# Two attention layers on one core: turned blocks loaded by whole sequences in rows of 2 KB

## The reference, cut to what matters

```python
x = x + L0_xattn(layernorm(x), ctx, ctx, ...)   # 16 heads of 8
x = x + L0_ffn(layernorm(x), ...)               # 8 experts, top 2
x = x + L1_xattn(layernorm(x), ctx, ...)        # 16 heads of 64
x = x + L1_ffn(layernorm(x), ...)
```

## Time and profile before

| | |
|---|---|
| median of three runs | 915.78 us (908.65 to 916.7) |
| profiled execution | 913.91 us, span 912.3 us |
| TensorE matmul busy | 828.5 us, 91% |
| ScalarE / VectorE busy | 74% / 70% |
| mean granted TensorE clock | 0.974 of full |
| bytes moved by DMA | 171.93 MB, 60.0% of the engines' time on SP's queue |

### The profile page before, as it was taken

The page is one execution under the profiler, slowest core; times in us unless marked ns, Lnnn a source line. Parts: engine busy times, 40 slices in busy tenths (PEclk is TensorE's granted clock), DMA queues, the critical chain, the costliest instruction groups (busy, mean ns, idle before and its releaser), DMA issues.

```text
span 912.3 us, 28139 instructions
## 1 busy us (share of the span) xinstructions
PE 828.5 (91%) x7885; PEld 734.4 (80%) x7885; DVE 638.7 (70%) x2052; ACT 673.3 (74%) x2662; POOL 453.2 (50%) x765
## 2 busy tenths in 40 slices
PE   5899999999998877999999678999999999999985
PEld 3677777777776766999999577889999999999974
DVE  5888887887887743222222578788898888888872
ACT  2999899899898852333334798899888888888860
POOL 3135445444454362111113777788777777776540
PEclk9999999999999997999999899999999999999987
DMA  5897667667767702222222198889899999999871
GB/s 169 247 244 217 204 208 227 201 211 228 219 208 240 196 30 78 70 71 70 70 70 64 64 253 253 253 240 269 246 241 232 238 238 237 240 239 240 240 233 41
DMA packets 160451, 171.93 MB, mean 188 GB/s; under 512 B 16052, under 2 KB 139318, under 8 KB 160374
## 3 DMA queue, kind: packets, MB, share of 16 engines
q1 hardware_dynamic: 153474, 156.77, 60.0%
q0 software_dynamic: 6112, 13.90, 5.7%
q10 hardware_dynamic: 788, 0.39, 0.2%
HBM read 90.87 MB, written 80.13 MB: 187 GB/s over the span
## 4 chain that ended last, share of the span: by engine, by line
PE 67%; DMA 9%; issue 8%; DVE 6%; SPq 4%; POOL 3%; ACT 3%; another core or an unknown queue 0%; POOLq 0%; DVEq 0%; ACTq 0%
PE bank L1233 8%; PE bank L1420 8%; PE bank L1392 7%; PE bank L1399 7%; PE bank L1442 5%; PE bank L1516 4%; PE bank L1432 4%; PE bank L1225 4%; DMA PTC<-turned_blocks 3%; PE bank L1506 3%; PE bank L1187 3%; PE bank L1344 3%; PE bank L1304 2%; PE bank L1521 2%; ACT PR L699 2%
## 5 line engine op out<-in xcount | busy, mean ns | idle before, releaser
L699 ACT ACTIVATE PR<-PR,nmx 128x128 f32<-128x128 f32 x512 | 198.4, 393 | 13.7 <-DVE nmx L898 13.6
L699 ACT ACTIVATE PR<-bank,nmx 128x128 f32<-128x128 f32 x512 | 188.0, 432 | 0.4 <-DVE nmx L898 0.4
L347 POOL TENSOR_TENSOR PR<-PR,rden 128x512 f32<-128x512 f32 x128 | 133.1, 1052 | 50.4 <-DVE rden L903 49.8
L699 ACT ACTIVATION_READ_ACCUMULATOR PR<-bank,nmx 128x1 f32 x512 | 139.6, 273 | 0.0
L1420 PE MATMUL bank<-XCT,wqk 128*128 128x128 f32 x832 | 104.6, 280 | 10.0 <-ACT XCT L687 9.7
L793 ACT ACTIVATE H<-bank 128x512 f32<-128x512 f32 x70 | 41.8, 597 | 92.3 <-PE bank L1392 92.3
L1420 PEld LDWEIGHTS bank<-XCT,wqk 128*128 128x128 f32 x832 | 98.3, 193 | 13.5 <-ACT XCT L687 10.5
L699 ACT ACTIVATION_READ_ACCUMULATOR PR<-PR,nmx 128x1 f32 x512 | 98.2, 192 | 0.0
L1187 PEld LDWEIGHTS bank<-ident,PR 128*128 128x128 f32 x512 | 60.2, 141 | 39.6 <-issue 38.1
L1065 DVE STREAM_TRANSPOSE BT<-PR 128x512 f32<-128x512 f32 x128 | 89.7, 701 | 2.3 <-POOL PR L347 1.5
L898 DVE TENSOR_REDUCE nmx<-bank 128x4 f32<-128x512 f32 x128 | 86.2, 673 | 4.5 <-PE bank L1225 3.5
(11 more groups left out here) (186 smaller groups left out, 1986.1 us busy)
## 6 DMA issues: line engine op xcount, KB each, us to landing
turned_blocks<-BT SPq DMA_DIRECT2D x64, 512.0 KB
PTC<-turned_blocks SPq DMA_DIRECT2D x256, 128.0 KB, 4.2
second_layer_values<-wide SPq DMA_DIRECT2D x32, 512.0 KB
wide<-second_layer_values SPq DMA_DIRECT2D x32, 512.0 KB
expert_outputs<-HF SPq DMA_DIRECT2D x32, 256.0 KB
expert_outputs<-HF SPq DMA_DIRECT2D x64, 128.0 KB
KBD<-expert_outputs SPq DMA_DIRECT2D x64, 128.0 KB
QS<-expert_outputs SPq DMA_DIRECT2D x32, 256.0 KB
```

Of the source, the lines that this page charges most:

```text
L347: nc.gpsimd.tensor_tensor(unit, unit, rden[:, p, G * g:G * g + G].unsqueeze(2).broadcast_to([P, G, P]), ALU.mult).then_inc(s["nm"], 1)
L699: last = nc.scalar.activation(PR[:, g, j * P:(j + 1) * P], scored, ACT.Exp, bias=nmx[:, p, h:h + 1], accum_out=den[:, p, h:h + 1])
```

## The change

`BT`, `PTC` and the DRAM buffer get one layout for the whole sequence: for each block column j, all 16 heads follow each other (2 KB). A half is then four pieces of 1 KB in a row, so each store has rows of 1 KB (512 in place of 128), strided by 2 KB on both sides. The loads are four in place of eight for a sequence, each of 256 KB with rows of 2 KB (128 rows, as before). They wait for both stores and for all products with v of the sequence that used the buffer before, and count on `pt0` alone. TensorE's `values(p, 0)` thus waits for the whole sequence, and the wait on `pt1` falls. The count of instructions on the compute engines stays the same.

```diff
-        bt_dram = nc.dram_tensor("turned_blocks", (2, 2, P, 2 * G * P), FP32, kind="Internal").ap()
+        bt_dram = nc.dram_tensor("turned_blocks", (2, P, 4 * G * P), FP32, kind="Internal").ap()
-        PTC = sb("PTC", [P, 2, 2, 4, 2 * G, 32])
+        PTC = sb("PTC", [P, 2, 4, NH, 32])
-        BT = sb("BT", [P, 2, 2 * G * P])
+        BT = sb("BT", [P, 4, NH * 32])
             def store_blocks(m, p, half):
-                wait_apart(sp, (c["bt"], NU * m + 2 * half + 2), (c[f"pt{half}"], 64 * (m - 1)))
-                sp.dma_start(bt_dram[p, half], BT[:, half, :]).then_inc(c[f"bw{half}"], 16)
-            def load_turned(m, p, half):
-                wait_apart(sp, (c[f"bw{half}"], 16 * (m + 1)), (c["pv"], NU * (m - 2) + 2 * half + 2))
+                wait_apart(sp, (c["bt"], NU * m + 2 * half + 2), (c["pt0"], 64 * (m - 1)))
+                columns = slice(2 * G * 32 * half, 2 * G * 32 * half + 2 * G * 32)
+                sp.dma_start(bt_dram[p].rearrange("r (j c) -> r j c", j=4)[:, :, columns], BT[:, :, columns]).then_inc(c[f"bw{half}"], 16)
+            def load_turned(m, p):
+                wait_apart(sp, (c["bw0"], 16 * (m + 1)), (c["bw1"], 16 * (m + 1)), (c["pv"], NU * (m - 1)))
                 for j in range(4):
-                    sp.dma_start(PTC[32 * j:32 * j + 32, p, half, :, :, :].rearrange("a i h b -> a i (h b)"),
-                                 bt_dram[p, half].rearrange("(i a) (j c) -> j a i c", a=32, j=4)[j]).then_inc(c[f"pt{half}"], 16)
+                    sp.dma_start(PTC[32 * j:32 * j + 32, p, :, :, :].rearrange("a i h b -> a i (h b)"),
+                                 bt_dram[p].rearrange("(i a) (j c) -> j a i c", a=32, j=4)[j]).then_inc(c["pt0"], 16)
 # SP, step1
-                    load_turned(n - 1, q, 0)
-                    load_turned(n - 1, q, 1)
+                    load_turned(n - 1, q)
 # VectorE, turn_unit
-                    nc.vector.transpose(BT[:, g // 2, :].rearrange("p (j h b) -> p h j b", j=4, b=32)[:, G * (g % 2):G * (g % 2) + G],
+                    nc.vector.transpose(BT[:].rearrange("p j (h b) -> p h j b", b=32)[:, G * g:G * g + G],
 # TensorE, values and step1
-                                      V1[:, p, 2 * (G * pair + j) + r, :], PTC[:, p, pair, :, G * r + j, :], start=True, stop=True)
+                                      V1[:, p, 2 * (G * pair + j) + r, :], PTC[:, p, :, 2 * G * pair + G * r + j, :], start=True, stop=True)
-                    wait(pe, c["pt1"], 64 * (n - 1))
```

## The result

The changed kernel takes 949.39 us (median of three runs, 948.47 to 950.88) against 915.78: a ratio of 1.0393, 95% interval 1.0309 to 1.0476. It is slower, and by 33.6 us where my forecast (926) had 10.2; the time lies outside my range. The profiled execution has a span of 949.2 us and a mean granted clock of 0.958 of full (before 912.3 and 0.974).

The account below looks back on a forecast made before the run. TensorE bounds late steps; early ones also wait for turned-block loads. Late 3 plus early 7 us plus 1.5 us of slowed clock took 913.9 to 925.4 profiled, 927.3 by the median; forecast 926, range 920 to 932 (0.43).

Parts of the forecast that it names:

- Stores of 1 KB rows: Stores of turned blocks: shorter rows at 58 ns a packet make each store land 0.6 us later.
- The rate of the loads: Loads of turned blocks with 2 KB rows: 270 GB/s, 3.9 us for 1 MB, with 355 and 212 as ends.
- one side of the ports: Rival, chance 0.16: neighbouring loads to partitions 0 to 63 hinder each other, all at 212 GB/s, 938 to 940 us.
- my 1.5 us around the data: Turned-block loads: time beside the data itself, from a 128 KB transfer on an idle queue, 2.0 us less 0.46.
- Early steps: Second layer, 540 to 620 us: later blocks are paid at once, 0.8 us a step, 9 steps, 7 us.
- the second kind: Early step where half 0's loads wait for their store behind the values' load: products end 2.1 us later.
- the first kind: Early step where half 1's loads start once its store has landed: products end at 613.2, 1.0 us later.
- the lower clock: TensorE's matmuls after one more long stall run slowed, about 1.5 us in two groups.
- rows pay: Rival, chance 0.28: 2 KB load rows at 355 GB/s pay for the wait, early steps 3 us, late none, 917 to 919.
- Late steps: Some 20 steps after 640 us: loads 0.3 us late, paid by half, 0.15 us a step, 3 us.
- The slack of 0.85 us: Late step: half 1's last load lands at 716.5, TensorE comes to half 1 at 717.35, in time by 0.85 us.
- The turn and TensorE's reads at other strides: VectorE's block writes and TensorE's block reads at changed strides: bound at 0 to 3%, taken as 0.

Follow-up runs that it names:

- the first experiment: The changed kernel's layout and 1 KB store rows, but with eight loads, waits and products by halves as in the kernel before: 915.08 us, 0.9995.

## Why the prediction was wrong

The direction was right, and so was the mechanism: four issues a sequence; the first one behind both stores; stalls for the turned blocks that grow early and appear late, ahead of all 32 products; the lateness paid every second step. Of the sizes:

**Stores of 1 KB rows**: I took +0.6 us of landing, from 58 ns a packet. Against the run with the same waits and 4 KB rows (2.76 us from the store's issue to the first load) the changed kernel has 3.33: +0.57. Right in size, though the packets went at 342 GB/s and not at the 280 that I had named. With the waits by half it costs nothing, as the first experiment shows.

**The rate of the loads**, the first term that was mis-sized: "I take 270 GB/s, with 355 and 212 as the ends." Measured 217 (medians of 208 to 222 over twelve steps). From first issue to last landing I had 6.8 us (5.4, and the tail of 1.4), and it took 7.75. The rows for it stood in the prediction: the 212 GB/s of the stretch with a full queue was the changed kernel's regime, and 270, read where two transfers to different halves were in flight, was not. The rival "one side of the ports" (0.16) had this and gave 938 to 940, still 9 us short.

The Trainium skill ("SBUF — State Buffer", Door 1: The DMA port swizzle) says that partitions 0 to 63 reach the same 8 of 16 ports as 0 to 31, and 64 to 127 the other 8; half of its full 435 GB/s would be an estimate of 218 GB/s. The runs agree: 208 to 222 GB/s to 32 neighbours, 319 to 379 to all partitions, no change in the full queue with the layout in DRAM. On two loads to different halves the same page ("SBUF — State Buffer", "Can I just issue two DMAs to hit both halves?") says that they serialize, with 6% gained. The order 0, 2, 1, 3 agrees roughly: 224 to 242 GB/s. What makes them serialize no run here shows.

Nor did I price the source: the loads' slow start (160 GB/s in a window where the unbroken layout has 352) is part of the 7.75 us, and my 1.5 us around the data came from a load of the experts' inputs.

**Early steps**, the second, and the larger: "The mean is 1.55, by half 0.8 us a step, for 9 steps 7 us." It took 15.0. In both kinds of step it took 7.6 us from the first load's issue to the last landing (614.90 - 607.31; in the second kind the products start 7.59 us after the first issue) in place of 5.4, and the rest is in two parts that I had priced too low. SP's timeline of the kernel after, second kind:

```profile
611.92 2.72 SPq L535 DMA_DIRECT2D turned_blocks<-BT  x2
620.28 1.75 SPq L541 DMA_DIRECT2D PTC<-turned_blocks  x4
```

From the first of two stores to the first load it is 8.36 us where I had 7.1 (617.0 - 609.87): these stores lie behind the values' load, which lies behind loads that still run at half rate. And in the first kind the stall is so long that the clock falls: from the store of half 1 (603.97) to the end of the products (618.63) it takes 14.7 us where the prediction had 11.3, of which 1.8 us is the transfers (10.9 in place of 9.1 to the last landing) and 1.5 us the products at 3.68 us in place of 2.2. I had counted the lower clock once, with 1.5 us in all, though the earlier trace rows shows it behind a single stall of 1.86 us; the long stalls after the change are 2.7 to 3.3 us, one every second step, and behind each of those in this execution the products are slow. I hadn't asked what the clock does if my own stalls come true.

**The wait by itself** was under-priced as well, independent of the rate. My case "rows pay" had 917 to 919 us at 355 GB/s, some 4 us over before. With loads at 324 to 359 GB/s and the change's waits the run was at 1.0146, 13 us. The prediction costed two kinds of step with their loads and left out the first products, which stand at the end of a transfer with nothing else to do (+4.1 us, with the caveat above), and the last three steps, which have less TensorE work, as the early ones do: +5.9 us in the change, +5.6 with SP's wait alone, +2.1 with TensorE's alone. That is a term that I never wrote.

**Late steps**: I took 0.15 us a step, 3 us; 10.0 us measured, 0.5 a step. With the measured rate in my own working it would have come out: at 212 GB/s I had the last landing 1.2 us late, 0.6 a step. The slack of 0.85 us was real and is spent: the run with both waits and the old transfers starts its products 7.47 us after the first issue (718.70 to 726.17) with no stall, and the changed kernel, with 0.57 us more for the store and at least 0.3 more for the loads, has 1 us of stall. I had named growth of over 0.3 us in a late step as a sign of being wrong, and it came.

**The turn and TensorE's reads at other strides**: I took 0; the turn has 701 ns in both, and the experiment with the stores and layout alone gives 0.9995.

## What to carry to other kernels

Before transfers are joined, look at what overlaps them in the old form: here the smaller loads ran under the landing of a store, and one condition that asks for both stores took that away, for 23 of 40 per mille, and put the store's short rows on the path, which had been free. Price a loop's transfers by the row in which the queue is in the state that the change makes, with the same partitions on the far side, not by the mean of the rows at hand; and cost each part of a pipeline that is short of other work (the first step, the early ones, the last ones) by itself, with the clock that the new stalls will bring.

## What the runs showed of the hardware

- Loads of 256 KB to 32 neighbouring partitions ran at 208 to 222 GB/s in a full queue with rows of 2 KB (medians of windows), and the loads of 128 KB at 212 with rows of 1 KB; to all 128 partitions with rows of 2 KB at 319 to 379, to every fourth at 269 to 362. The row's length hardly mattered. With the order 0, 2, 1, 3 it was 224 to 242.
- Reading a load's 256 KB from an unbroken stretch of DRAM in place of 2 KB out of every 8 left that rate as it was, but the data came sooner: 352 GB/s in place of 160 in the 0.7 us from 1.5 us after the first issue, and 7.11 us in place of 7.75 until all four had landed.
- Stores of 512 rows of 1 KB went at 342 GB/s and cost the kernel nothing where there was slack; the issue took 0.52 us in place of 0.32, and the first load behind such a store came 3.33 us after it in place of 2.76.
- Issuing a load to every fourth partition took 0.66 us in place of 0.43.
- A turn of 32 x 32 blocks that reads its input at a stride of 4 elements took 1123 ns in place of 701.
- Of one kernel on several chips the time differed by 3% (885.5 to 914.1 us), while ratios stayed close: SP's wait with TensorE's had 1.0269 on the fastest chip and 1.0251 on another, the loads to all partitions 1.0138 and 1.0146.
